# First products row by row: fc1's weights loaded in chunks over all partitions, the first two chunks multiplied for row 0 and then for row 1

## The chip, the cores and the metric

The kernel runs on one NeuronCore of one Trainium2 chip. The metric is the device time of one execution in microseconds (us); less is better. Beside it stands the span of the profile, from the first to the last instruction of the core.

## What is computed

`x` is 32 rows of 256 tokens with 256 features. Each row has an expert number. All arrays are float32.

```
h        = gelu(einsum('bnd,hd->bnh', x, fc1_w) + fc1_b)         # fc1_w: 1024 x 256
shared   = einsum('bnh,sh->bns', h, fc2_w) + fc2_b               # 192 outputs
expert_x = einsum('bnh,bph->bnp', h, experts_w[indices]) + be    # 64 outputs
return x + concatenate([shared, expert_x], axis=-1)
```

## The kernel before

**Blocks.** A block is two rows (R = 2), that is 512 tokens, and there are 16 blocks. Each fp32 operand is split into a high part (HI, written by ScalarE as fp32r) and a low part (LO, the difference, mostly written by VectorE, for the hidden values by GpSimd), and a product is three matmuls: HI x HI, HI x LO and LO x HI. fc1 of blocks 0 and 1 is computed plainly, in eight chunks of 128 hidden features (`conv_chunk`, L961, six matmuls of 512 columns each: two halves `d` of the features times three terms). From block 2 on a scheme with sums of blocks is used (L985). fc2 (`fc2_units`, L1017, L1019, L1021) takes two chunks of hidden values, a pair, at a time.

**Order.** Nothing is scheduled by a tool: each engine has its own instruction stream, written by hand, and waits on semaphores. The streams of TensorE (PE), ScalarE (ACT), VectorE (DVE), GpSimd (POOL) and SyncE (SP) are what stands in the functions below.

**The opening.** TensorE first runs `warm` (L930), products of the identity that feed nothing. It transposes block 0 of `x` (`x0_banks`, into `tr_ps`), then the first half of fc1's weights (`w1_bank(0, d)`, four chunks, into `acc_ps`), then the bias, then runs chunk 0 (`first_chunk`, L968), transposes the second half of the weights (`w1_bank(1, d)`, into `tr_ps`), and runs chunks 1 to 7 without a break. Behind them stands `fc2_units(0, 0, 0, 8)`, whose first matmul waits for the first pair of hidden values. Between TensorE's steps ScalarE splits off the high parts (`x0_high` L417, `w1_high` L430) and VectorE the low ones (`x0_low` L646, `w1_low` L659).

**The first pair of hidden values.** ScalarE applies the gelu to chunks 0 and 1 (`conv_chunk` L522; chunk 0 waits for `b1_ready`, which VectorE's copy of the transposed bias sets, L826), and later rounds the pair to its high part (`conv_high(0)`, L510). GpSimd makes the low part (`pair_lo`, L353, semaphore `h_lo`). Ahead of `conv_high(0)` ScalarE and VectorE have to get fc2's weights ready in turns: VectorE transposes a quarter (`w2_square`, L682), ScalarE writes its high part (`w2_high`, L440), VectorE its low part (`w2_low`, L690). `w2_square(0)` stands behind `w1_low(1, 1)` in VectorE's stream. After fc2's weights come the experts' weights (L701, L709) and block 1 of `x` (L720, and its low part L737, `x1_lo`), for which TensorE's `conv_chunk(K)` waits behind `fc2_units(0, 0, 0, 8)`.

**Loads.** The queue of SP issues the two rows of block 0, waits for row 0 (`x0_loaded[0]`), and issues the second half of fc1's weights, four DMAs of 32 partitions each, and then fc2's. ACT's queue issues the expert numbers, the first half of fc1's weights in the same form, and fc1's bias.

The opening of TensorE's stream in the source:

```
for d in range(D):
    w1_bank(0, d)
pe.wait_ge(b1_loaded, 16)
nc.tensor.transpose(fc1_ps[:, 3, 0:K], b1_in[:, :], ident[0:K, 0:K]).then_inc(b1_tr, 1)
first_chunk()
pe.wait_ge(w1_loaded[1], 16 * Q)
```

## Time and profile before

| | |
|---|---|
| median of 3 runs | 363.62 us (363.24 to 364.08) |
| the profiled execution's own time | 363.34 us |
| its span | 361.5 us |
| TensorE (PE) matmuls busy | 356.4 us (99%) |
| PE weight loads (PEld) busy | 350.3 us (97%) |
| ScalarE (ACT) busy | 243.6 us (67%) |
| VectorE (DVE) busy | 224.0 us (62%) |
| GpSimd (POOL) busy | 222.2 us (61%) |
| mean granted TensorE clock | 0.998 |

The profile shows one execution. Its span is 1.84 us shorter than its own time, and that time is 0.28 us under the median. Busy times of different engines overlap. A row of a timeline gives the start from the beginning of the span, the length, the engine, the line of the kernel, and what is written from what; a row with "x6" stands for six instructions in succession, and its length runs from the first start to the last end. The engine is idle ahead of an instruction where square brackets say so, and behind the arrow stands what ended the idle time.

### The profile page before, as it was taken

The page shows a single profiled execution, that of the slowest core. Times are in us where ns is not written, and L with a number is a line of the kernel's source. Part 1 is how long each engine was busy: PE and PEld are TensorE (multiplying, and loading weights), DVE is VectorE, ACT ScalarE, POOL GpSimd, SP SyncE. Part 2 cuts the span into 40 slices and gives each one's busy share as a digit, 9 for nine tenths or more (in the row PEclk, how much of TensorE's full clock was granted, in tenths as well). Part 3 has the DMA queues.
Part 4 walks back from the last instruction along what each step waited for, and adds up shares of the span by engine and source line. Part 5 has one row for each costly group of instructions (what it writes and reads, how often), then busy time and mean ns, then how long its engine had stood idle before and what let it go on. Part 6 is the DMA issues. An engine that isn't in the chain of part 4 may idle for free.

```text
span 361.5 us, 7842 instructions
## 1 busy us (share of the span) xinstructions
PE 356.4 (99%) x2863; PEld 350.3 (97%) x2863; DVE 224.0 (62%) x367; ACT 243.6 (67%) x410; POOL 222.2 (61%) x100
## 2 busy tenths in 40 slices
PE   8999999999999999999999999999999999999996
PEld 6898999999999999999999999999999999999996
DVE  1797993937758285683937658395673938653241
ACT  3794865757849576694857759576794857757560
POOL 0079824676655677565676655677565577655381
PEclk9999999999999999999999999999999999999999
DMA  8869856361703426044261603526052321403011
GB/s 202 183 160 117 156 143 150 126 160 45 175 22 116 127 69 173 31 124 89 82 160 52 168 25 109 132 82 162 29 140 74 94 91 58 126 18 100 2 58 58
DMA packets 70447, 37.86 MB, mean 105 GB/s; under 512 B 43530, under 2 KB 70410, under 8 KB 70410
## 3 DMA queue, kind: packets, MB, share of 16 engines
q1 hardware_dynamic: 69792, 36.85, 40.8%
q10 hardware_dynamic: 618, 0.53, 0.6%
q8 instruction: 22, 0.36, 0.4%
q14 instruction: 15, 0.12, 0.1%
HBM read 28.97 MB, written 8.39 MB: 103 GB/s over the span
## 4 chain that ended last, share of the span: by engine, by line
PE 95%; issue 2%; POOL 1%; ACT 1%; DVE 0%; POOLq 0%
PE fc_ps L985 37%; PE acc_ps L1017 16%; PE acc_ps L1021 16%; PE acc_ps L1019 16%; PE fc_ps L961 6%; PE fc_ps L930 1%; POOL ht L353 1%; PE tr_ps L924 1%; PE fc_ps L968 1%; ACT ht L510 0%; ACT gelu L536 0%; DVE work L794 0%; DVE resid L819 0%; ACT w1t L430 0%; PE acc_ps L924 0%
## 5 line engine op out<-in xcount | busy, mean ns | idle before, releaser
L353 POOL TENSOR_TENSOR ht<-gelu,ht 128x1024 fp32r<-128x1024 f32 x60 | 144.5, 2408 | 121.3 <-ACT ht L510 121.3
L985 PE MATMUL fc_ps<-xt,w1t 128*128 128x256 f32 x1176 | 173.2, 283 | 0.0
L985 PEld LDWEIGHTS fc_ps<-xt,w1t 128*128 128x128 f32 x1176 | 155.3, 192 | 0.1
L1017 PE MATMUL acc_ps<-w2t,ht 128*128 128x256 f32 x512 | 144.9, 283 | 0.2 <-POOL ht L353 0.2
L1019 PE MATMUL acc_ps<-w2t,ht 128*128 128x256 f32 x512 | 144.9, 283 | 0.0
L1021 PE MATMUL acc_ps<-w2t,ht 128*128 128x256 f32 x512 | 144.9, 283 | 0.0
L1017 PEld LDWEIGHTS acc_ps<-w2t,ht 128*128 128x128 f32 x512 | 98.3, 192 | 0.6 <-POOL ht L353 0.3
L1019 PEld LDWEIGHTS acc_ps<-w2t,ht 128*128 128x128 f32 x512 | 98.3, 192 | 0.3
L1021 PEld LDWEIGHTS acc_ps<-w2t,ht 128*128 128x128 f32 x512 | 98.3, 192 | 0.0
L510 ACT ACTIVATE ht<-gelu 128x1024 fp32r<-128x1024 f32 x64 | 68.0, 1062 | 3.3
L496 ACT ACTIVATE work<-fc_ps 128x512 f32<-128x512 f32 x28 | 16.8, 600 | 57.4 <-PE fc_ps L985 57.4
L778 DVE TENSOR_TENSOR work<-fc_ps,work 128x512 f32<-128x512 f32 x28 | 19.4, 691 | 54.6 <-PE fc_ps L985 45.8
L346 POOL TENSOR_TENSOR resid<-resid,bias 128x1024 f32<-128x1024 f32 x16 | 38.9, 2432 | 1.5 <-DMA resid<-in_x 0.8
L787 DVE TENSOR_TENSOR work<-fc_ps,work 128x512 f32<-128x512 f32 x28 | 19.2, 687 | 32.0 <-PE fc_ps L985 32.0
L361 POOL TENSOR_TENSOR xt<-work,xt 128x1024 fp32r<-128x1024 f32 x14 | 33.6, 2402 | 7.7 <-ACT xt L500 7.7
L450 ACT ACTIVATE w2t<-tr_ps 128x512 fp32r<-128x512 f32 x32 | 18.8, 590 | 29.0 <-PE acc_ps L1021 29.0
L536 ACT ACTIVATE gelu<-work,b 128x512 f32<-128x512 f32 x56 | 37.1, 712 | 0.7 <-DVE work L794 0.7
L794 DVE TENSOR_TENSOR work<-fc_ps,work 128x512 f32<-128x512 f32 x28 | 19.3, 691 | 12.8 <-PE fc_ps L985 11.2
L548 ACT ACTIVATE gelu<-work,b 128x256 f32<-128x256 f32 x56 | 25.2, 501 | 0.0
L709 DVE TENSOR_TENSOR w2t<-tr_ps,w2t 128x512 fp32r<-128x512 f32 x32 | 22.0, 690 | 4.7 <-ACT w2t L450 3.2
L802 DVE TENSOR_TENSOR work<-fc_ps,work 128x512 f32<-128x512 f32 x28 | 19.1, 683 | 7.2 <-PE fc_ps L985 7.2
L553 ACT ACTIVATE gelu<-fc_ps,b 128x256 f32<-128x256 f32 x56 | 23.3, 469 | 0.0
(57 smaller groups left out, 279.5 us busy)
## 6 DMA issues: line engine op xcount, KB each, us to landing
pieces<-in_L_cond_experts_w SPq DMA_DIRECT2D x128, 64.0 KB, 2.0
out<-resid SPq DMA_DIRECT2D x32, 256.0 KB, 3.0
pieces<-in_x SPq DMA_DIRECT2D x60, 128.0 KB, 3.6
resid<-in_x SPq DMA_DIRECT2D x15, 512.0 KB, 4.1
bias<-in_L_cond_experts_b SPq DMA_DIRECT2D x32, 32.0 KB, 2.9
w_piece<-in_L_cond_fc_w SPq DMA_DIRECT2D x4, 256.0 KB, 4.5
w_piece<-in_L_cond_fc_w SPq DMA_DIRECT2D x4, 192.0 KB, 5.0
resid<-in_x SPq DMA_DIRECT2D x2, 256.0 KB, 3.4
```

The costliest lines, as they stand in the source:

```text
L346: nc.gpsimd.tensor_tensor(rows, rows, bias[:, par, :, :].unsqueeze(2).to_broadcast([P, R, T, OUT]), ALU.add).then_inc(resid_ready, 1)
L353: nc.gpsimd.tensor_tensor(ht[:, slot, LO, :, :].rearrange("p k t -> p (k t)"), gelu[:, q % GELUS, :, :].rearrange("p k t -> p (k t)"), ht[ ...
L361: nc.gpsimd.tensor_tensor(xt[:, n % 2, X_T1:X_T4 + 1, LO, :], t_sum, xt[:, n % 2, X_T1:X_T4 + 1, HI, :].bitcast(FP32), ALU.subtract).then_ ...
L510: nc.scalar.activation(ht[:, q % PAIRS, HI, :, :].rearrange("p k t -> p (k t)"), gelu[:, q % GELUS, :, :].rearrange("p k t -> p (k t)"), A ...
L536: nc.scalar.activation(gelu[:, q % GELUS, j, :], upper[:, j, :], ACT.Gelu, bias=b1[:, k:k + 1]).then_inc(up_gelu, 1)
L548: nc.scalar.activation(gelu[:, q % GELUS, j, SEQ:2 * SEQ], c22[:, j, :], ACT.Gelu, bias=b1[:, k:k + 1]).then_inc(c22_gelu, 1)
L553: nc.scalar.activation(gelu[:, q % GELUS, j, 0:SEQ], fc1_ps[:, BANK_A[t % 2], j * SEQ:(j + 1) * SEQ], ACT.Gelu, bias=b1[:, k:k + 1]).then_ ...
L709: nc.vector.tensor_tensor(expert_columns(LO, ks), tr_ps[:, half, :].rearrange("p (k b c) -> p b k c", k=HALF, b=R), expert_columns(HI, ks) ...
L985: last = nc.tensor.matmul(fc1_ps[:, dst, j * SEQ:(j + 1) * SEQ], w1t[:, w, wv, ms], xt[:, n % 2, o, xv, :], start=(fresh and j == 0 and at ...
L1017: nc.tensor.matmul(dst, h_hi_t, w_hi, start=(r == 0 and u % (2 * T) == 0), stop=True, skip_group_check=True)
L1019: nc.tensor.matmul(dst, h_hi_t, w_lo, start=False, stop=True, skip_group_check=True)
L1021: last = nc.tensor.matmul(dst, h_lo_t, w_hi, start=False, stop=True, skip_group_check=True)
```

## The change

The loads of fc1's first half become four DMAs, one for each chunk, each over all 128 partitions (`load_w1_chunk`): chunks 0 and 1 from ACT's queue, chunks 2 and 3 from SP's queue, right behind block 0. The bias and the expert numbers move to SP's queue. The second half of the weights keeps its four DMAs.

A bank of transposed weights now holds two chunks with both halves of the features (`w1_bank(half, l)`), where it held four chunks with one half. A bank of transposed `x` holds one row (`x0_banks(b)`), where it held one half of the features of both. `x0_high`, `x0_low`, `w1_high` and `w1_low` follow: there are as many of them and they are as large as before, in another order. `first_chunk(c, b)` computes chunk c for row b, six matmuls of 256 columns, and runs for chunks 0 and 1, first for row 0, then for row 1. Ten of the 30 warming products are gone. On ScalarE the second of the two `w1_high` of the second half moves behind the gelu of chunk 1.

```diff
+    w1_chunks = fc1_w.rearrange("(q k c) d -> k q c d", q=Q, c=S)
...
+        def x0_row(v, b):
+            return xt0[:, :, v, b * SEQ:(b + 1) * SEQ]
+        def x0_bank(b):
+            return tr_ps[:, b, :].rearrange("p (d t) -> p d t", d=D)
+        W1_ORDER = ((0, 1), (1, 0))
+        def w1_slots(half, l, v):
+            cols = slice(2 * half * P, (2 * half + 2) * P)
+            if l == 0:
+                return w1t[:, W_A11:W_A12 + 1, v, cols]
+            return w1t[:, W_A22:W_A21 + 1:W_A21 - W_A22, v, cols]
+        def w1_rows(half, l):
+            return (acc_ps, tr_ps)[half][:, l, :].rearrange("p (d c) -> p d c", d=D)
...
+        w1_loaded = [sem(f"w1_loaded{n}") for n in range(3)]
         w1p_loaded = sem("w1p_loaded")
...
-        def load_w1(queue, half):
-            ks = slice(half * HALF, (half + 1) * HALF)
-            for q in range(Q):
-                queue.dma_start(w1_in[S * q:S * (q + 1), ks, :], w1_v[q][:, ks, :])\
-                    .then_inc(w1_loaded[half], 16)
+        def load_w1_chunk(queue, k):
+            queue.dma_start(w1_in[:, k, :], w1_chunks[k]).then_inc(w1_loaded[k // 2], 16)
...
                 sp.dma_start(resid[:, 0, ts, :], x_blocks[0][:, ts, :]).then_inc(x0_loaded[b], 16)
+            load_w1_chunk(sp, 2)
+            load_w1_chunk(sp, 3)
+            sp.dma_start(b1_in[:, :].rearrange("k (q c) -> k q c", q=Q),
+                         fc1_b.rearrange("(q k c) -> k q c", q=Q, c=S))\
+                .then_inc(b1_loaded, 16)
+            sp.dma_start(index_sb[:, :], index.rearrange("(o n) -> o n", o=1))\
+                .then_inc(index_loaded, 16)
             sp.wait_ge(x0_loaded[0], 16)
-            load_w1(sp, 1)
+            for q in range(Q):
+                sp.dma_start(w1_in[S * q:S * (q + 1), HALF:K, :], w1_v[q][:, HALF:K, :])\
+                    .then_inc(w1_loaded[2], 16)
...
-            def x0_high(d):
-                act.wait_ge(x0_tr, d + 1)
-                nc.scalar.activation(xt0[:, d, HI, :], tr_ps[:, d, :], ACT.Copy)\
-                    .then_inc(x0_hi, 1)
-            def w1_slots(half, d, v):
-                cols = slice(2 * half * P, (2 * half + 2) * P)
-                if d == 0:
-                    return w1t[:, W_A11:W_A21 + 1:W_A21 - W_A11, v, cols]
-                return w1t[:, W_A12:W_A22 + 1, v, cols]
-            def w1_high(half, d):
-                act.wait_ge(w1_tr, D * half + d + 1)
-                src = (acc_ps, tr_ps)[half][:, d, :].rearrange("p (l c) -> p l c", l=2)
-                nc.scalar.activation(w1_slots(half, d, HI), src, ACT.Copy).then_inc(w1_hi, 1)
+            def x0_high(b):
+                act.wait_ge(x0_tr, b + 1)
+                nc.scalar.activation(x0_row(HI, b), x0_bank(b), ACT.Copy).then_inc(x0_hi, 1)
+            def w1_high(half, l):
+                act.wait_ge(w1_tr, 2 * half + l + 1)
+                nc.scalar.activation(w1_slots(half, l, HI), w1_rows(half, l), ACT.Copy)\
+                    .then_inc(w1_hi, 1)
...
-            act.dma_start(index_sb[:, :], index.rearrange("(o n) -> o n", o=1))\
-                .then_inc(index_loaded, 16)
-            load_w1(act, 0)
-            act.dma_start(b1_in[:, :].rearrange("k (q c) -> k q c", q=Q),
-                          fc1_b.rearrange("(q k c) -> k q c", q=Q, c=S))\
-                .then_inc(b1_loaded, 16)
+            load_w1_chunk(act, 0)
+            load_w1_chunk(act, 1)
             act.wait_ge(ident_ready, 1)
             nc.scalar.activation(gelu[:, 0, 0, 0:1], ident[:, 0:1], ACT.Gelu)\
                 .then_inc(gelu_loaded, 1)
             act.wait_ge(gelu_loaded, 1)
-            for d in range(D):
-                x0_high(d)
-            for d in range(D):
-                w1_high(0, d)
+            x0_high(0)
+            w1_high(0, 0)
+            x0_high(1)
+            w1_high(0, 1)
             act.wait_ge(b1_ready, 1)
             conv_chunk(0)
             w1_high(1, 0)
+            conv_chunk(1)
             w1_high(1, 1)
-            conv_chunk(1)
...
-            def x0_low(d):
-                dve.wait_ge(x0_hi, d + 1)
-                nc.vector.tensor_tensor(xt0[:, d, LO, :], tr_ps[:, d, :],
-                                        xt0[:, d, HI, :].bitcast(FP32), ALU.subtract)\
-                    .then_inc(x0_lo, 1)
...
-            def w1_low(half, d):
-                dve.wait_ge(w1_hi, D * half + d + 1)
-                src = (acc_ps, tr_ps)[half][:, d, :].rearrange("p (l c) -> p l c", l=2)
-                nc.vector.tensor_tensor(w1_slots(half, d, LO), src,
-                                        w1_slots(half, d, HI).bitcast(FP32), ALU.subtract)\
+            def x0_low(b):
+                dve.wait_ge(x0_hi, b + 1)
+                nc.vector.tensor_tensor(x0_row(LO, b), x0_bank(b), x0_row(HI, b).bitcast(FP32),
+                                        ALU.subtract).then_inc(x0_lo, 1)
+            def w1_low(half, l):
+                dve.wait_ge(w1_hi, 2 * half + l + 1)
+                nc.vector.tensor_tensor(w1_slots(half, l, LO), w1_rows(half, l),
+                                        w1_slots(half, l, HI).bitcast(FP32), ALU.subtract)\
                     .then_inc(w1_lo, 1)
...
-            for d in range(D):
-                x0_low(d)
-            for d in range(D):
-                w1_low(0, d)
+            x0_low(0)
+            w1_low(0, 0)
+            x0_low(1)
+            w1_low(0, 1)
             dve.wait_ge(b1_tr, 1)
             nc.vector.tensor_copy(b1[:, :], fc1_ps[:, 3, 0:K]).then_inc(b1_ready, 1)
-            for d in range(D):
-                w1_low(1, d)
+            w1_low(1, 0)
+            w1_low(1, 1)
             w2_square(0)
...
                 pe.wait_ge(x0_loaded[b], 16)
-                for d in range(D):
-                    last = transposes(tr_ps[:, d, b * SEQ:(b + 1) * SEQ],
-                                      [feature_chunk(resid[:, 0, b * T + t, :], d)
-                                       for t in range(T)])
-                    if b == R - 1:
-                        last.then_inc(x0_tr, 1)
-            def w1_bank(half, d):
-                transposes((acc_ps, tr_ps)[half][:, d, :], [
-                    feature_chunk(w1_in[:, k, :], d)
-                    for k in range(half * HALF, (half + 1) * HALF)]).then_inc(w1_tr, 1)
+                transposes(tr_ps[:, b, :], [
+                    feature_chunk(resid[:, 0, b * T + t, :], d)
+                    for d in range(D) for t in range(T)]).then_inc(x0_tr, 1)
+            def w1_bank(half, l):
+                k = half * HALF + 2 * l
+                transposes((acc_ps, tr_ps)[half][:, l, :], [
+                    feature_chunk(w1_in[:, k + j, :], d)
+                    for d in W1_ORDER[l] for j in range(2)]).then_inc(w1_tr, 1)
...
-            def first_chunk():
-                def product(d, w, v):
-                    return nc.tensor.matmul(fc1_ps[:, 0, :], conv_operand(0, d, w), xt0[:, d, v, :],
-                                            start=(d == 0 and w == v), stop=(d == D - 1 and w == LO))
-                for d in range(D):
-                    pe.wait_ge(w1_hi, d + 1)
-                    product(d, HI, HI)
-                    pe.wait_ge(x0_lo, d + 1)
-                    product(d, HI, LO)
-                for d in range(D):
-                    pe.wait_ge(w1_lo, d + 1)
-                    last = product(d, LO, HI)
-                last.then_inc(conv_filled, 1)
+            def first_chunk(c, b):
+                for at, (w, v, d) in enumerate([(w, v, d) for w, v in ((HI, HI), (HI, LO), (LO, HI))
+                                                for d in range(D)]):
+                    if c == 0 and at == 0:
+                        pe.wait_ge(w1_hi, 1)
+                        pe.wait_ge(x0_hi, b + 1)
+                    if c == 0 and (w, v, d) == (HI, LO, 0):
+                        pe.wait_ge(x0_lo, b + 1)
+                    if c == 0 and (w, v, d) == (LO, HI, 0):
+                        pe.wait_ge(w1_lo, 1)
+                    last = nc.tensor.matmul(fc1_ps[:, c, b * SEQ:(b + 1) * SEQ],
+                                            conv_operand(c, d, w),
+                                            xt0[:, d, v, b * SEQ:(b + 1) * SEQ],
+                                            start=(b == 0 and at == 0), stop=True,
+                                            skip_group_check=True)
+                if b == R - 1:
...
             warm(WARM)
-            for b in range(R):
-                x0_banks(b)
-            warm(WARM // 2)
-            pe.wait_ge(w1_loaded[0], 16 * Q)
-            for d in range(D):
-                w1_bank(0, d)
+            x0_banks(0)
+            pe.wait_ge(w1_loaded[0], 32)
+            w1_bank(0, 0)
+            x0_banks(1)
+            first_chunk(0, 0)
             pe.wait_ge(b1_loaded, 16)
             nc.tensor.transpose(fc1_ps[:, 3, 0:K], b1_in[:, :], ident[0:K, 0:K]).then_inc(b1_tr, 1)
-            first_chunk()
-            pe.wait_ge(w1_loaded[1], 16 * Q)
-            for d in range(D):
-                pe.wait_ge(x0_lo, d + 1)
-                w1_bank(1, d)
-            conv_chunk(1)
+            first_chunk(1, 0)
+            pe.wait_ge(w1_loaded[1], 32)
+            w1_bank(0, 1)
+            first_chunk(0, 1)
+            first_chunk(1, 1)
+            pe.wait_ge(w1_loaded[2], 16 * Q)
+            pe.wait_ge(x0_lo, 1)
+            w1_bank(1, 0)
+            pe.wait_ge(x0_lo, 2)
+            w1_bank(1, 1)
+            pe.wait_ge(w1_lo, 2)
             conv_chunk(2)
             conv_chunk(3)
-            pe.wait_ge(w1_lo, 4)
+            pe.wait_ge(w1_lo, 3)
             conv_chunk(4)
             conv_chunk(5)
+            pe.wait_ge(w1_lo, 4)
             conv_chunk(6)
             conv_chunk(7)
```

TensorE's stream from its start to the first fc2 matmul, before (`w_in` is fc1's weights as loaded, `w1t` the split weights, `resid` block 0 of `x`; in these rows `tr_ps`, `acc_ps` and `fc_ps` are PSUM banks):

```order
L930 MATMUL fc_ps<-ident 128x256 x20
L924 MATMUL tr_ps<-ident,resid 128x128 x8
L930 MATMUL fc_ps<-ident 128x256 x10
L924 MATMUL acc_ps<-ident,w_in 128x128 x8
L1037 MATMUL fc_ps<-ident,b_in 128x8
L968 MATMUL fc_ps<-xt,w1t 128x512 x6
L924 MATMUL tr_ps<-ident,w_in 128x128 x8
L961 MATMUL fc_ps<-xt,w1t 128x512 x42
```

The same place in the changed kernel:

```order
L937 MATMUL fc_ps<-ident 128x256 x20
L931 MATMUL tr_ps<-ident,resid 128x128 x4
L931 MATMUL acc_ps<-ident,w_in 128x128 x4
L931 MATMUL tr_ps<-ident,resid 128x128 x4
L982 MATMUL fc_ps<-xt,w1t 128x256 x6
L1046 MATMUL fc_ps<-ident,b_in 128x8
L982 MATMUL fc_ps<-xt,w1t 128x256 x6
L931 MATMUL acc_ps<-ident,w_in 128x128 x4
L982 MATMUL fc_ps<-xt,w1t 128x256 x12
L931 MATMUL tr_ps<-ident,w_in 128x128 x8
L966 MATMUL fc_ps<-xt,w1t 128x512 x36
```

The first half of the weights is now transposed in two parts: one ahead of row 1 of `x`, the other behind the products of chunks 0 and 1 for row 0. 24 products of 256 columns take the place of 12 of 512, and 36 products of 512 stand ahead of fc2 where 42 stood.

ScalarE's stream from its first instruction on block 0 to its first on fc2's weights (L440, in the changed kernel L459), before:

```order
L417 ACTIVATE xt<-tr_ps 128x512 [waits x0_tr,gelu_loaded]
L417 ACTIVATE xt<-tr_ps 128x512 [waits x0_tr]
L430 ACTIVATE w1t<-acc_ps 128x2x256 [waits w1_tr] x2
L522 ACTIVATE gelu<-fc_ps,b 128x512 [waits conv_filled,b1_ready]
L430 ACTIVATE w1t<-tr_ps 128x2x256 [waits w1_tr] x2
L522 ACTIVATE gelu<-fc_ps,b 128x512 [waits conv_filled]
L440 ACTIVATE w2t<-acc_ps 128x2x192 [waits w2_sq] x2
```

The same place in the changed kernel:

```order
L444 ACTIVATE xt<-tr_ps 128x2x256 [waits x0_tr,gelu_loaded]
L448 ACTIVATE w1t<-acc_ps 128x2x256 [waits w1_tr]
L444 ACTIVATE xt<-tr_ps 128x2x256 [waits x0_tr]
L448 ACTIVATE w1t<-acc_ps 128x2x256 [waits w1_tr]
L541 ACTIVATE gelu<-fc_ps,b 128x512 [waits conv_filled,b1_ready]
L448 ACTIVATE w1t<-tr_ps 128x2x256 [waits w1_tr]
L541 ACTIVATE gelu<-fc_ps,b 128x512 [waits conv_filled]
L448 ACTIVATE w1t<-tr_ps 128x2x256 [waits w1_tr]
L459 ACTIVATE w2t<-acc_ps 128x2x192 [waits w2_sq] x2
```

Ahead of the first gelu stand the same four instructions in another order; the gelu of chunk 1 now stands between the two `w1_high` of the second half. VectorE's stream changes only in the order of its first four instructions; the copy of the bias (L826) still stands behind them, and `w1_low` of the second half behind the copy.

## Rows read from the trace of the kernel before

**Rows 1.** The page: the span, and busy time of each engine

```profile
span 361.5 us, 7842 instructions
PE 356.4 (99%) x2863; PEld 350.3 (97%) x2863; DVE 224.0 (62%) x367; ACT 243.6 (67%) x410; POOL 222.2 (61%) x100
```

**Rows 2.** PE busy (x), clock, DMA share, GB/s from 44 to 345 us

```profile
44.00:345.00 301.00, 301.00 (x2509) 1.00 0.36 98
```

**Rows 3.** Timeline of PE, the opening

```profile
1.53 4.12 PE L930 MATMUL fc_ps<-ident 128*128 128x256 bf16 x20 [1.53 <-POOL ident L379]
5.49 1.12 PE L924 MATMUL tr_ps<-ident,resid 128*128 128x128 f32 x8
6.45 1.25 PE L930 MATMUL fc_ps<-ident 128*128 128x256 bf16 x10
...
8.59 0.22 PE L1037 MATMUL fc_ps<-ident,b_in 8*128 8x8 f32 x1
8.86 1.83 PE L968 MATMUL fc_ps<-xt,w1t 128*128 128x512 f32 x6
```

**Rows 4.** Timeline of PEld: first half's end, fc2's first load, chunk 8's first

```profile
11.36 9.42 PEld L961 LDWEIGHTS fc_ps<-xt,w1t 128*128 128x128 f32 x42
20.82 0.19 PEld L1017 LDWEIGHTS acc_ps<-w2t,ht 128*128 128x128 f32 x1
...
23.80 0.19 PEld L961 LDWEIGHTS fc_ps<-xt,w1t 128*128 128x128 f32 x1
```

**Rows 5.** Timeline of POOL: the low part of the first pair

```profile
18.16 2.41 POOL L353 TENSOR_TENSOR ht<-gelu,ht 128x1024 fp32r<-128x1024 f32 x1 [16.68 <-ACT ht L510]
```

**Rows 6.** Timeline of DVE, the opening

```profile
7.10 0.69 DVE L646 TENSOR_TENSOR xt<-tr_ps,xt 128x512 fp32r<-128x512 f32 x1 [7.10 <-ACT xt L417]
...
10.05 0.16 DVE L826 COPY b<-fc_ps 128x8 f32<-128x8 f32 x1
12.00 1.29 DVE L659 TENSOR_TENSOR w1t<-tr_ps,w1t 128x512 fp32r<-128x512 f32 x2 [1.80 <-ACT w1t L430]
13.21 1.04 DVE L682 STREAM_TRANSPOSE acc_ps<-w_piece 128x384 f32<-128x384 f32 x2
...
22.86 0.68 DVE L737 TENSOR_TENSOR xt<-tr_ps,xt 128x512 fp32r<-128x512 f32 x1
```

**Rows 7.** Timeline of ACT, the opening

```profile
6.47 0.60 ACT L417 ACTIVATE xt<-tr_ps 128x512 fp32r<-128x512 f32 x1 [1.44 <-PE tr_ps L924]
...
10.79 0.69 ACT L522 ACTIVATE gelu<-fc_ps,b 128x512 f32<-128x512 f32 x1 [1.49 <-PE fc_ps L968]
11.38 1.08 ACT L430 ACTIVATE w1t<-tr_ps 128x512 fp32r<-128x512 f32 x2
...
13.82 0.95 ACT L440 ACTIVATE w2t<-acc_ps 128x384 fp32r<-128x384 f32 x2
...
17.02 1.06 ACT L510 ACTIVATE ht<-gelu 128x1024 fp32r<-128x1024 f32 x1
```

**Rows 8.** Timeline of SP's queue, DMAs issued

```profile
0.75 0.95 SPq L286 DMA_DIRECT2D resid<-in_x  x2
3.76 1.76 SPq L236 DMA_DIRECT2D w_in<-in_L_cond_fc_w  x4
5.57 1.93 SPq L291 DMA_DIRECT2D w_piece<-in_L_cond_fc_w  x4
```

**Rows 9.** DMA issues to 40 us (median us to landing); GB/s of each us

```profile
GB/s 0 18 239 321 296 238 237 237 234 214 236 212 246 149 217 235 105 44 115 215 188 155 125 86 128 162 243 239 188 200 152 57 56 53 55 78 148 156 214 167
...
w_piece<-in_L_cond_fc_w SPq DMA_DIRECT2D x4, 192.0 KB, 5.0
resid<-in_x SPq DMA_DIRECT2D x2, 256.0 KB, 3.4
w_in<-in_L_cond_fc_w ACTq DMA_DIRECT2D x4, 128.0 KB, 4.1
```

**Rows 10.** The chain that ended last: six products of 256 columns

```profile
45.90 0.72 PE fc_ps L985 x6
```

More of the change, by code:

```diff
@@ L120, in cond_mlp_residual @@
         stored = [sem(f"stored{n}") for n in range(2)]
-        w1_loaded = [sem(f"w1_loaded{n}") for n in range(2)]
+        w1_loaded = [sem(f"w1_loaded{n}") for n in range(3)]
         w1p_loaded = sem("w1p_loaded")
@@ L964, in conv_chunk @@
                 last.then_inc(conv_filled, 1)
-            def first_chunk():
-                def product(d, w, v):
-                    return nc.tensor.matmul(fc1_ps[:, 0, :], conv_operand(0, d, w), xt0[:, d, v, :],
-                                            start=(d == 0 and w == v), stop=(d == D - 1 and w == LO))
-                for d in range(D):
-                    pe.wait_ge(w1_hi, d + 1)
-                    product(d, HI, HI)
-                    pe.wait_ge(x0_lo, d + 1)
-                    product(d, HI, LO)
-                for d in range(D):
-                    pe.wait_ge(w1_lo, d + 1)
-                    last = product(d, LO, HI)
-                last.then_inc(conv_filled, 1)
+            def first_chunk(c, b):
[14 more added lines that the diff above has]
+                if b == R - 1:
+                    last.then_inc(conv_filled, 1)
             def product(n, g, dst, w, o, fresh):
```

5 lines of the change are left out of this document (removed).

## The prediction

> **What bounds the kernel now.** I read the page first. TensorE is busy 99% of a span of 361.5 us, and no other engine more than 67% [rows 1]. The windows say where the missing 1% is not: from 44 to 345 us TensorE is busy for all 301 us at the full clock [rows 2]. The change touches only the first 12 us or so. So whatever it does must move the moment at which TensorE comes into that full stretch, and the time of the kernel moves by as much. TensorE's timeline of the opening comes next [rows 3]: it cannot start before 1.53 us, it warms itself for 4.12 us, transposes from 5.49, fills 1.25 us with ten more warming products, and the first product that counts begins at 8.86. That is the hole that the change works on.
>
> The question then is who is late next. TensorE's weight loads show chunks 1 to 7 from 11.36 for 9.42 us, so to 20.78, and the first load of fc2 at 20.82, with no wait shown [rows 4]. But what that fc2 matmul waits for, `h_lo`, comes from GpSimd's instruction at 18.16 of 2.41 us, which ends at 20.57 [rows 5]. The margin is 0.25 us. The next wait, chunk 8 on `x1_lo`, is as tight: the load stands at 23.80 [rows 4], VectorE's last low part ends at 22.86 + 0.68 = 23.54 [rows 6]. Two chains run side by side here, TensorE's own and that of ScalarE, VectorE and GpSimd, and they meet within 0.25 us.
>
> What sets the second chain is read on VectorE and ScalarE. From 13.21 VectorE and ScalarE work by turns on fc2's weights: ScalarE's first copy of them is at 13.82, after the first of VectorE's two transposes from 13.21 [rows 6, 7]. At 17.02, 3.81 us after 13.21, ScalarE rounds the first pair, in 1.06 us, and at 18.16 GpSimd begins [rows 5, 7]. The products that these steps need are long finished: chunks 1 to 3 take 18 of the 42 loads from 11.36. So I call T the start of `w2_square(0)`, 13.21 us; `h_lo` follows at T + 7.36 and `x1_lo` at T + 10.33. T itself follows from the gelu of chunk 0 at 10.79: 0.59 later ScalarE's first high part (11.38), 0.62 later VectorE's first low part (12.00), and two of those at a pitch of 0.60 give 13.21 [rows 6, 7].
>
> **The change, the loads.** SP issued one DMA of a row in about 0.47 us and had issued its first of fc1's second half at 3.76, when row 0 had landed; fc2's weights follow at 5.57 to 7.50 [rows 8]. Four more DMAs of about 0.45 fit between 1.70 and 3.5, so SP's queue is hardly later, and ACT's has four fewer. fc2's weights take 5.0 us to land [rows 9], so they are there by about 12.5, or 13 if all slips by half a microsecond, and T' below is later than that. Chunks 0 and 1 are issued by about 1.65; such a DMA took 4.1 us with four of them in the queue [rows 9], so both land by about 5.3 where 5.97 is wanted. The GB/s row says the same by bytes: 874 KB had moved by 5 us (18 + 239 + 321 + 296), and row 0 with the two chunks is 512 KB. I cost the loads at nothing.
>
> The Trainium skill ("DMA: Bandwidth & Descriptors", Issuing engines are not separate DMA queues) says that DMAs of all issuing engines run on the same 16 DMA engines and interleave, so that two queues save issue time only. No row here splits the two, and the sum goes by the bytes.
>
> **TensorE's new opening**, step by step. Eight transposes took 1.12 us and the next work began 0.96 after their start, so a pitch is 0.12 and one lasts 0.28; the first copy on ScalarE (6.47) came 0.10 after the sixth, the last that it needs [rows 3, 7]. A product of 256 columns costs 0.12 (six in 0.72) [rows 10], one of 512 costs 9.42 / 42 = 0.224 [rows 4]. ScalarE: 0.60 a copy, pitch 0.49; VectorE: 0.69, pitch 0.60, and 0.03 after ScalarE (6.47 + 0.60 to 7.10) [rows 6, 7].
>
> Row 0's four transposes from 5.49 end at 6.13, ScalarE's `x0_high(0)` starts at 6.23. The four of chunks 0 and 1 end at 6.61, `w1_high(0, 0)` runs from 6.72 to 7.31. TensorE has transposed row 1 by 7.1 and starts its first product at about 7.35, 1.5 us before the old one. VectorE: `x0_low(0)` at 6.86, `w1_low(0, 0)` from 7.46 to 8.15. TensorE waits for that ahead of its fifth product, does two until 8.43, the bias (between 0.12 and 0.22 by its length [rows 3]; I take 0.14), and the six of chunk 1 until 9.29. Only now come the transposes of chunks 2 and 3, which before were done in one go with the others: the last ends at 9.29 + 0.36 + 0.28 = 9.93.
>
> **TensorE's side.** From 9.29: four transposes (0.48), 12 products (1.44), eight transposes (0.96) give 12.17 for the start of chunk 2. Before, it was 11.36 + 6 x 0.224 = 12.70. TensorE gains 0.55 us and would be at fc2 at 20.27. In it the split of 12 products of 512 columns into 24 of 256 costs 24 x 0.12 - 12 x 0.224 = 0.2.
>
> **The other side.** ScalarE's `w1_high(0, 1)` starts at 10.03, ends 10.63; VectorE's `w1_low(0, 1)` 10.66; the copy of the bias stands behind it, 0.60 later as before, at 11.26, and takes 0.16 [rows 6]. Only then may ScalarE start the gelu of chunk 0: 11.45, where it was 10.79. 0.59 later the first high part of the second half, 12.04; 0.49 later the gelu of chunk 1, which now stands between the two, 12.53; 0.59 later the second high part, 13.12 to 13.72; VectorE's last `w1_low` 13.75, and T' = 14.35. That is 1.14 after T: 0.66 from the bias standing behind a late bank, 0.48 from the gelu in between.
>
> **Sum.** `h_lo` at 20.57 + 1.14 = 21.71, so fc2 starts at about 21.75 instead of 20.82: +0.93. TensorE will have waited some 1.5 us for it. `x1_lo` at 23.54 + 1.14 = 24.68 against 23.80 + 0.93 = 24.73 adds nothing. The hand-overs may be a few hundredths shorter, as PE to ScalarE; I take +0.9. On the profiled execution: 363.34 + 0.9 = 364.24. That execution was 0.28 below the median of the three, 363.62, and against the median the number is **364.5 us**. The bounds of the parts (bias, hand-overs, an unseen wait for the high parts in the queue of ScalarE) make 364.1 to 364.9 for this case. A measurement of this kernel tells some 0.2% (0.73 us) from no change, so the forecast lies only a little above that bound.
>
> **The rivals.**
> - *The turns have slack (0.20).* ScalarE's and VectorE's steps behind T may absorb some of the 1.14, or the bias comes earlier than I have it. For it: the interval of 3.81 us is more than any one engine's work in it. Against: the copy at 13.82 follows its transpose within hundredths. With half of the delay gone, 0.57 - 0.25 = +0.3: 363.9 us, and no change to be measured.
> - *TensorE's gain is kept (0.07): faster.* If `h_lo` came by 20.23, fc2 would start at 20.27 and the kernel would take 363.62 - 0.55 = 363.1. This decides only if T' is 12.87 or earlier, 1.5 us before what I work out. For it: the first product starts 1.5 us earlier. Against: the gelu of chunk 0 is the gate, and that waits for the bias copy.
> - *Late chunks (0.07).* Chunks 0 and 1 now compete with row 0 from the start. If they land at 6.7 instead of before 5.97, all steps shift by 0.7: 365.2. For it: row 0 itself took 3.4 us [rows 9]. Against: the bytes above. In this case the change does not do what it says, since no product starts much before 8.1.
> - *The clock (0.06).* Twenty warming products took 4.12 us, ten later ones 1.25 [rows 3]: a pitch of 0.2 against 0.11, so 1.2 GHz first and 2.4 GHz later, after TensorE had been working. Ten warming products are gone and a wait of 1.5 us is new. If the clock fell in that wait and the next twenty products of 256 columns ran at the lower level, as twenty did at the start, each would cost 0.09 more: +1.8, in all 366.3. Against: waits of some tenths in the old opening left no slow product behind, but none was as long. The Trainium skill ("TensorE: Matmul & The Clock Gate", Part 1: The HAM clock gate) says that an idle TensorE goes back to 1.2 GHz and activity releases it; the trace agrees on the release at the start, and shows no fall.
>
> **The numbers.** Forecast 0.60, slack 0.20, gain kept 0.07, late chunks 0.07, clock 0.06. The range from 363.3 to 365.5 leaves out the kept gain, the clock and a part of the late chunks. Of the forecast's 0.60 about 0.42 lies above +0.73 us, with the late chunks and the clock slower has 0.56; faster has 0.08; the rest, 0.36, is the same.
>
> **What would show it.** In the changed profile: the first product near 7.35, chunk 2 near 12.2, the gelu of chunk 0 near 11.45, the transpose of fc2's weights near 14.35, an idle time of about 1.5 us on TensorE ahead of fc2's first load with GpSimd's low part as its releaser, and the full stretch from there on as before. I would be wrong if that idle time is missing, if the gelu of chunk 0 starts before 11 us, or if the wait for `w1_loaded` stands in the opening.

## The result, and the profile after

The changed kernel takes 372.68 us (median of 4 runs, 372.25 to 372.75), the kernel before in the same session 363.82 (363.24 to 364.08). The ratio is 1.0243, with a 95% interval from 1.0226 to 1.0261: 8.9 us slower. I had forecast slower, by 0.9 us. The direction holds, and the size is wrong by a factor of ten.

The page of the changed kernel, to be read against [rows 1]:

```profile
span 370.5 us, 7849 instructions
PE 357.9 (97%) x2865; PEld 351.7 (95%) x2865; DVE 224.0 (60%) x367; ACT 243.5 (66%) x410; POOL 223.2 (60%) x100
PEclk9699999999999999999999999999999999999999
```

TensorE's busy time grew by 1.5 us, the span by 9.0. So TensorE waits, and the clock line says where: in the second slice, which ends at 18.5 us. The waits of TensorE in the changed kernel, the two lists of PEld and PE (engine, what it waited for, total, times, longest):

```profile
PEld acc_ps L931 <- DMA w_in<-in_L_cond_fc_w: 6.6, 1, 6.6
PEld acc_ps L1027 <- POOL ht L380: 1.9, 2, 1.6
...
PE acc_ps L931 <- DMA w_in<-in_L_cond_fc_w: 6.3, 1, 6.3
```

The first line is new. TensorE waits 6.6 us for chunks 0 and 1 to land. The second is the wait that I had forecast at 1.5 us; its longest is 1.6. The timeline of the changed kernel, against [rows 3 to 7]:

```profile
0.74 1.72 ACTq L255 DMA_DIRECT2D w_in<-in_L_cond_fc_w  x2
...
1.75 1.32 SPq L255 DMA_DIRECT2D w_in<-in_L_cond_fc_w  x2
...
5.78 0.91 PE L931 MATMUL tr_ps<-ident,resid 128*128 128x128 f32 x4
...
13.02 0.73 PEld L931 LDWEIGHTS acc_ps<-ident,w_in 128*128 128x128 f32 x4 [6.58 <-DMA w_in<-in_L_cond_fc_w]
...
19.55 0.69 ACT L541 ACTIVATE gelu<-fc_ps,b 128x512 f32<-128x512 f32 x1 [0.83 <-PE fc_ps L982]
...
20.19 2.85 PEld L966 LDWEIGHTS fc_ps<-xt,w1t 128*128 128x128 f32 x13
...
22.43 1.04 DVE L689 STREAM_TRANSPOSE acc_ps<-w_piece 128x384 f32<-128x384 f32 x2
...
27.39 2.39 POOL L380 TENSOR_TENSOR ht<-gelu,ht 128x1024 fp32r<-128x1024 f32 x1 [25.90 <-ACT ht L529]
...
29.82 0.19 PEld L1027 LDWEIGHTS acc_ps<-w2t,ht 128*128 128x128 f32 x1 [1.57 <-POOL ht L380]
```

Both loads on ACT's queue were issued by 2.46 us, and TensorE could start on them at 13.0. The four transposes of row 0 are done by 6.7, and between the two TensorE does nothing. The windows of PE in the changed kernel (busy (x), granted clock, DMA share, GB/s) show the two other things that matter, what the DMA engines did and what the clock did:

```profile
3.00:4.00 1.00, 1.00 (x6) 1.00 0.89 293
4.00:5.00 1.00, 1.00 (x7) 1.00 0.28 98
5.00:6.00 1.00, 1.00 (x7) 1.00 0.53 140
...
8.00:10.00 2.00, 0.00 (x0) 0.96 1.08 203
10.00:12.00 2.00, 0.00 (x0) 0.50 1.09 182
12.00:14.00 2.00, 0.98 (x5) 0.50 0.34 72
14.00:16.00 2.00, 2.00 (x10) 0.50 0.28 76
16.00:18.00 2.00, 2.00 (x15) 0.84 0.54 153
```

Between 4 and 5 us all four chunk loads are under way, and yet the sixteen DMA engines are busy only 28% of the time and move 98 GB/s; the kernel before moved 296 [rows 9], at a share of 1.13:

```profile
4.00:5.00 1.00, 1.00 (x7) 1.00 1.13 296
```

Queues that have work and engines that idle: the work is on few of them. And after some microseconds without a matmul the granted clock falls to 0.50, which is 1.2 GHz; it is back in the window from 16 to 18 (0.84 on average, so at about 16.6), that is, it stays low for the first 3.6 us of real work.

### The profile page after: what moved, and what is told of

It reads as the page before. It is cut to its first block, busy times and chain, and to the rows that moved or that the text cites. A ratio compares the mean times of both kernels' runs of the same rounds, so it can differ in the third digit from the quotient of the medians.

```text
span 370.5 us, 7849 instructions
## 1 busy us (share of the span) xinstructions
PE 357.9 (97%) x2865; PEld 351.7 (95%) x2865; DVE 224.0 (60%) x367; ACT 243.5 (66%) x410; POOL 223.2 (60%) x100
## 4 chain that ended last, share of the span: by engine, by line
PE 89%; DMA 3%; issue 2%; POOL 2%; ACT 2%; DVE 1%; ACTq 0%; DVEq 0%; POOLq 0%
PE fc_ps L995 37%; PE acc_ps L1027 16%; PE acc_ps L1031 16%; PE acc_ps L1029 16%; PE fc_ps L966 3%; DMA w_in<-in_L_cond_fc_w 3%; POOL ht L380 2%; PE fc_ps L982 1%; ACT ht L529 1%; ACT gelu L541 0%; PE acc_ps L931 0%; ACT w2t L459 0%; DVE acc_ps L689 0%; ACTq L255 0%; ACT w1t L448 0%
## 5 line engine op out<-in xcount | busy, mean ns | idle before, releaser
L373 POOL TENSOR_TENSOR resid<-resid,bias 128x1024 f32<-128x1024 f32 x16 | 39.7, 2481 | 0.0
```

The lines of the kernel that those rows point to most:

```text
L373: nc.gpsimd.tensor_tensor(rows, rows, bias[:, par, :, :].unsqueeze(2).to_broadcast([P, R, T, OUT]), ALU.add).then_inc(resid_ready, 1)
```

## The experiments

**Theories.** A: the source of a chunk load has four steps in its outermost dimension (`k q c d`, q = 4), and such a DMA runs on four of the sixteen engines only. All four chunks pile up there, and whatever else passes these engines waits with them. B: ACT's queue is starved while SP's queue has a backlog (SP no longer pauses behind the two rows). C: a DMA over 128 partitions of this kind is slow in itself.

**e1_quarters: the loads in the old form.** The computation stays as changed.

```diff
-        def load_w1_chunk(queue, k):
...
-            queue.dma_start(w1_in[:, k, :], w1_chunks[k]).then_inc(w1_loaded[k // 2], 16)
+        def load_w1_pair(queue, l):
+            ks = slice(2 * l, 2 * l + 2)
+            for q in range(Q):
+                queue.dma_start(w1_in[S * q:S * (q + 1), ks, :], w1_v[q][:, ks, :])\
+                    .then_inc(w1_loaded[l], 16)
...
```

Pair 0 comes from ACT's queue and pair 1 from SP's, and TensorE waits for 64 where it waited for 32; the same holds for every kernel below that loads in this form.

> The changed kernel, but chunks 0 and 1 come from ACT's queue and chunks 2 and 3 from SP's as four DMAs of 32 partitions x 2 chunks each, the form that the kernel before uses, in place of one DMA of 128 partitions per chunk. Theory A (the new form of the chunk loads has four steps in its outermost source dimension and so runs on four of the sixteen DMA engines): the loads land by about 5.5 us, the wait of 6.3 us is gone, and what is left is the predicted lateness of the chain of ScalarE, VectorE and GpSimd: 364.5 us (364.1 to 364.9), with the gelu of chunk 0 near 11.5 and fc2's first load near 21.7. Theory B (ACT's queue is starved while SP's queue has a backlog, whatever the form): chunks 0 and 1 still land near 12 to 13 us, 371 to 373 us.

Measured: 365.0 us (364.73 to 365.36, 10 runs), ratio 1.0032 (1.0021 to 1.0044), against a before of 363.88. 7.7 of the 8.9 us are gone by the form of four loads alone. B as it stands is out, since the queues and the bytes in them are the same. What is left is 0.32% or 1.2 us; it is mostly my chain, which e6_sixteen below shows with the loads on time, but TensorE still waits 0.87 us for the chunks here and starts on them at 6.34, where I had 5.97. The timeline of e1_quarters:

```profile
6.34 0.56 PEld L931 LDWEIGHTS acc_ps<-ident,w_in 128*128 128x128 f32 x4 [0.87 <-DMA w_in<-in_L_cond_fc_w]
...
12.02 0.69 ACT L542 ACTIVATE gelu<-fc_ps,b 128x512 f32<-128x512 f32 x1 [0.83 <-PE fc_ps L982]
12.60 0.59 ACT L449 ACTIVATE w1t<-tr_ps 128x512 fp32r<-128x512 f32 x1
12.66 8.06 PEld L966 LDWEIGHTS fc_ps<-xt,w1t 128*128 128x128 f32 x36
...
14.90 1.04 DVE L689 STREAM_TRANSPOSE acc_ps<-w_piece 128x384 f32<-128x384 f32 x2
...
22.29 0.19 PEld L1027 LDWEIGHTS acc_ps<-w2t,ht 128*128 128x128 f32 x1 [1.56 <-POOL ht L381]
```

Against the changed kernel the first transposes of chunks come 13.02 - 6.34 = 6.68 us earlier. From there to chunk 2 it takes 12.66 - 6.34 = 6.32 us, where the changed kernel took 20.19 - 13.02 = 7.17: another 0.85, which is the slow clock (e8_warm50 tests this). Together that is 7.5, and the spans differ by 7.6.

**e2_before_chunk_form: the new form in the old kernel.** Nothing else changes.

```diff
-            load_w1(act, 0)
+            for k in range(HALF):
+                act.dma_start(w1_in[:, k, :], w1_chunks[k]).then_inc(w1_loaded[0], 16)
```

> The kernel before, with nothing changed but the form of the loads of fc1's first half: four DMAs from ACT's queue, one for each chunk over 128 partitions, in place of four of 32 partitions x 4 chunks. 
Measured: 374.25 us (4 runs), ratio 1.0286 (1.0266 to 1.0305). The form costs the old kernel 10.4 us by itself, though SP's queue paused as ever, and B allowed 1 us: as the whole cause it is out a second time. The size was above my 367.5 to 369. The wait list of e2_before_chunk_form, a window, the clock line of its page and two rows of its timeline:

```profile
PEld acc_ps L926 <- DMA w_in<-in_L_cond_fc_w: 8.3, 1, 8.3
```

```profile
4.00:5.00 1.00, 1.00 (x7) 1.00 0.14 48
```

```profile
PEclk9789999999999999999999999999999999999999
```

```profile
16.58 1.59 PEld L926 LDWEIGHTS acc_ps<-ident,w_in 128*128 128x128 f32 x8 [8.31 <-DMA w_in<-in_L_cond_fc_w]
...
21.94 4.21 PEld L963 LDWEIGHTS fc_ps<-xt,w1t 128*128 128x128 f32 x19
```

I had left two things out. The first is the clock. In the kernel before the transposes of the first half start at 7.43 us and chunk 1 at 11.36 [rows 4], 3.93 later; here it is 21.94 - 16.58 = 5.36, and the clock line is below 9 in the second and third slice (9.3 to 27.9 us). The start is 9.15 later and the stretch 1.43 longer, together the 10.6 by which the spans differ. The second is that I had counted only the chunks and block 0 on the four engines. But if SP's later loads, fc1's second half and fc2's weights, use all sixteen, they pass through these four as well, and ACT's loads share with them. The changed kernel shows the sharing in the packets of ACT's queue (q10; number, MB, share of the engines), from 4 to 5, 5 to 6 and 8 to 9 us. SP issued the second half from 4.27 on:

```profile
q10 hardware_dynamic: 63, 0.06, 18.1%
...
q10 hardware_dynamic: 18, 0.01, 4.4%
...
q10 hardware_dynamic: 28, 0.03, 15.0%
```

So a part of B is true: SP's backlog does slow ACT's loads, but in e1_quarters, where they are not on few engines, it did not make them late by more than 0.4 us. How much of the delay the sharing makes was not tried by itself.

**e3_only_act_quarters: only chunks 0 and 1 in the old form.** Chunks 2 and 3 on SP's queue stay as changed.

```diff
-            load_w1_chunk(act, 0)
-            load_w1_chunk(act, 1)
+            for q in range(Q):
+                act.dma_start(w1_in[S * q:S * (q + 1), 0:2, :], w1_v[q][:, 0:2, :])\
+                    .then_inc(w1_loaded[0], 16)
```

> The changed kernel with chunks 0 and 1 on ACT's queue in four DMAs of 32 partitions, and chunks 2 and 3 on SP's queue left as one DMA of 128 partitions each. Theory A (four engines): chunks 0 and 1 land by about 5.5 to 6 us; chunks 2 and 3 share engines with the rows and land at about 9 us, where they are wanted at 9.3; the second half stands behind them on the same engines and may be 0 to 1.5 us late: 364.5 to 366. Theory B (starved behind SP's backlog): SP's queue is as in the changed kernel, so chunks 0 and 1 still land near 12 to 13 us: 371 to 373.

Measured: 368.13 us (366.32 to 369.19, 4 runs), ratio 1.0124 (1.0102 to 1.0145). B's 371 to 373 is missed, and so are A's 364.5 to 366. In the profiled execution, the fastest of the four at 366.32, TensorE waited 0.6 us for chunks 0 and 1, and for the bias, 4 KB behind the two chunk loads in SP's queue, 1.0 us:

```profile
PEld fc_ps L1047 <- DMA b_in<-in_L_cond_fc_b: 1.0, 1, 1.0
PEld acc_ps L932 <- DMA w_in<-in_L_cond_fc_w: 0.6, 1, 0.6
```

Two of the four chunk loads are enough to be felt, and by the small loads behind them too. The other three executions took 367.8 to 369.2 us with a mean granted clock of 0.995, where the profiled one has 1.000, so a stretch at the low clock is a part of their time. What they waited for was not profiled.

**e6_sixteen and e7_eight: the number of steps.** Destination, bytes, rows of 1 KB, queue and order are those of the changed kernel. Only the source is cut otherwise: 128 steps in the outermost dimension, or eight. fc1's rows then come in another order than the bias and fc2's weights want, so these two leave the function of the reference and serve for the time alone.

```diff
-    w1_chunks = fc1_w.rearrange("(q k c) d -> k q c d", q=Q, c=S)
+    w1_chunks = fc1_w.rearrange("(k p) d -> k p d", p=P)               # e6_sixteen
+    w1_chunks = fc1_w.rearrange("(e k c) d -> k e c d", e=8, c=16)     # e7_eight
```

> The changed kernel with only the source of the four chunk loads altered: each chunk takes 128 rows of fc1_w that lie together, so that the source has 128 steps in its outermost dimension and not four. Destination, bytes, rows of 1 KB, queue and order stay. The hidden features come in another order than the bias and fc2's weights want, so the output is not the reference's. Theory A (the outermost source dimension of four confines such a DMA to four engines): as e1_quarters, 364.7 to 365.4 us, no wait for the chunks beyond about 1 us. Theory C (a DMA of 128 partitions issued this way is slow in itself, or ACT's queue gets too small a share): as the changed kernel, 372 to 373 us.

> As e6_sixteen, but the source of each chunk has eight steps in its outermost dimension, of 16 rows each (again another order of the hidden features, so the output is not the reference's). Theory A: eight engines carry the chunk loads, half as many packets on each as with four: the chunks land between those of e6_sixteen (about 6 us) and those of the changed kernel (13 us), at 7 to 9.5 us; TensorE waits 0.5 to 2.5 us, the clock hardly falls; 365.5 to 368.5 us. Theory C: 372 to 373 us.

A chunk of the changed kernel is made of four groups of 32 rows of fc1's weights, one of e7_eight of eight groups of 16, spread as widely, and in e6_sixteen the 128 rows lie together. If it mattered how the rows are scattered in memory, and not how many steps there are, e7_eight should be no faster than the changed kernel.

Measured: e6_sixteen 364.8 us, ratio 1.0029 (1.0019 to 1.0039, 9 runs); e7_eight 366.89 us, ratio 1.0099 (1.0076 to 1.0121, 4 runs). C is out, since the shape of the destination stayed. The windows of e7_eight and then of e6_sixteen, in the microsecond in which the changed kernel had a DMA share of 0.28:

```profile
4.00:5.00 1.00, 1.00 (x7) 1.00 0.57 184
```

```profile
4.00:5.00 1.00, 1.00 (x7) 1.00 1.06 361
```

Four steps give a share of 0.28, eight 0.57, 128 steps 1.06: about 4, 8 and 16 parts of sixteen. The GB/s follow, 98, 184 and 361, and so does the time. In the changed kernel all four chunk loads were under way in that microsecond, so they are on the same few engines; spread over different ones they would show a share near 1.

The pages show the same without a window. In these kernels ACT's queue carries nothing but chunks 0 and 1, 256 rows of 1 KB, as two loads, and in e1_quarters as four. Its line in the pages of the changed kernel, e7_eight, e6_sixteen and e1_quarters, in this order:

```profile
q10 hardware_dynamic: 264, 0.26, 0.3%
...
q10 hardware_dynamic: 272, 0.26, 0.3%
...
q10 hardware_dynamic: 288, 0.26, 0.2%
...
q10 hardware_dynamic: 320, 0.26, 0.3%
```

Beyond the 256 packets of rows stand 8, 16, 32 and 64 more: 4, 8 and 16 for each load, and 16 for each load of the old form. Read as one closing packet from each engine that takes part, these are the engines of each load. The Trainium skill ("DMA: Bandwidth & Descriptors", Why a DMA increments its semaphore by 16 and not by 1) has the rule: a DMA uses as many engines as the largest number up to 16 that divides the sizes of the slowest dimension (other than one) of both its sides. For 128 partitions and a source of 4 x 32 x 256 that is four. By that rule, the trace agrees in all three forms.

**e8_warm50: what the slow clock cost.** The changed kernel with its slow loads, and TensorE kept at work while it waits.

```diff
             x0_banks(0)
+            warm(50)
             pe.wait_ge(w1_loaded[0], 32)
```

> The changed kernel with 50 more warming products behind the transposes of row 0, which keep TensorE busy for about 5.5 us of the wait for chunks 0 and 1. The loads are untouched, so the chunks land at 13 us as before; if the clock then stays at 2.4 GHz, the stretch from the first transposed chunk to chunk 2 takes 6.3 us as in e1_quarters and not 7.2: 0.9 us less than the changed kernel, 371.8 us. If the slower clock cost nothing there, 372.7 us.

Measured: 371.52 us (4 runs), ratio 1.0225 (1.0205 to 1.0244), against 1.0243. The timeline of e8_warm50:

```profile
12.88 0.56 PEld L931 LDWEIGHTS acc_ps<-ident,w_in 128*128 128x128 f32 x4 [0.71 <-DMA w_in<-in_L_cond_fc_w]
...
19.20 3.30 PEld L966 LDWEIGHTS fc_ps<-xt,w1t 128*128 128x128 f32 x15
```

The clock line of its page, where the changed kernel had a 6 in the second slice:

```profile
PEclk9999999999999999999999999999999999999999
```

The clock stayed up (0.999 on average over the span), and the stretch takes 6.32 us again, as in e1_quarters, and not 7.17. The two intervals overlap, so the time alone would not settle it; the timeline does. The spans, 369.5 against 370.5, differ by these 0.85 and the 0.14 by which the chunks came earlier.

**e4_gelu_behind and e5_order_restored: the two halves of my 1.14 us.** Both start from e1_quarters. e4 puts ScalarE's order back, e5 also moves the bias.

```diff
             w1_high(1, 0)
+            w1_high(1, 1)
             conv_chunk(1)
-            w1_high(1, 1)
...
-            w1_low(0, 1)
             dve.wait_ge(b1_tr, 1)
             nc.vector.tensor_copy(b1[:, :], fc1_ps[:, 3, 0:K]).then_inc(b1_ready, 1)
+            w1_low(0, 1)
```

The lines behind the "..." are e5's alone.

> e1_quarters with two places of the order changed: ScalarE's second high part of the second half again ahead of the gelu of chunk 1, and VectorE's copy of the bias ahead of the low part of chunks 2 and 3 instead of behind it. My chain (h_lo waits for the start of w2_square, that for the gelu of chunk 0 and the two high parts): the gelu of chunk 0 then waits for the end of chunk 0 for both rows, near 10.6 us, which is 0.8 to 0.9 earlier, and the gelu of chunk 1 no longer stands between, 0.5 less: w2_square(0) at 13.1 instead of 14.35, fc2's first load at 20.5 instead of 21.7: 1.2 us less than e1_quarters, 363.3 us, a little under the kernel before. Rival (the turns on fc2's weights have slack, so that the chain is not what TensorE waits for): no difference from e1_quarters beyond 0.2 us.

> e1_quarters with ScalarE's second high part of the second half put back ahead of the gelu of chunk 1; the copy of the bias stays where the change has it. In e1_quarters the first of these high parts starts at 12.60 us, 0.14 after TensorE has its bank ready, so the bias has almost nothing to give there, and the gelu in between costs 0.5. If so this kernel takes 0.4 to 0.6 us less than e1_quarters and is equal to e5_order_restored within 0.2 us: 364.4 to 364.6. If both places counted as in my prediction (0.66 for the bias, 0.48 for the gelu) it would stand halfway, and e5_order_restored would be lower than it by 0.6.

Measured: e5_order_restored 364.53 us, ratio 1.0016 (1.0006 to 1.0026, 12 runs), and then e4_gelu_behind, ratio 1.0014 (1.0005 to 1.0023, 11 runs; its median of 364.74 stands against a before of 364.12). Against e1_quarters the order on ScalarE gives 0.5 us by the medians and 0.18%, some 0.6 us, by the ratios, whose intervals just touch. The timeline of e4_gelu_behind settles it:

```profile
12.14 0.69 ACT L542 ACTIVATE gelu<-fc_ps,b 128x512 f32<-128x512 f32 x1 [0.83 <-PE fc_ps L982]
...
21.95 0.19 PEld L1027 LDWEIGHTS acc_ps<-w2t,ht 128*128 128x128 f32 x1 [1.10 <-POOL ht L381]
```

From the gelu of chunk 0 to fc2's first load it takes 21.95 - 12.14 = 9.81 us, where e1_quarters took 22.29 - 12.02 = 10.27: 0.46 less. The bias copy gives nothing on top. My 1.2 us for both together was wrong: e5's timeline shows what I had missed.

```profile
12.12 1.03 PEld L931 LDWEIGHTS tr_ps<-ident,w_in 128*128 128x128 f32 x8
...
12.91 1.08 ACT L449 ACTIVATE w1t<-tr_ps 128x512 fp32r<-128x512 f32 x2 [0.45 <-PE tr_ps L931]
```

ScalarE waits 0.45 us for TensorE's transposes of the second half, which now stand behind the products of row 1. With the bias out of the way TensorE's own order is the next gate. In e1_quarters these transposes had been ready only 0.14 us before ScalarE took them (the first bank at 11.82 + 3 x 0.12 + 0.28 = 12.46, ScalarE at 12.60), so moving the bias could give no more than that.

**e9_banks_first: that gate opened.** e5_order_restored, with the transposes ahead of row 1's products and ScalarE's two high parts ahead of the gelu of chunk 0.

```diff
             w1_bank(0, 1)
-            first_chunk(0, 1)
-            first_chunk(1, 1)
             pe.wait_ge(w1_loaded[2], 16 * Q)
             pe.wait_ge(x0_lo, 1)
             w1_bank(1, 0)
             pe.wait_ge(x0_lo, 2)
             w1_bank(1, 1)
+            first_chunk(0, 1)
+            first_chunk(1, 1)
...
+            w1_high(1, 0)
+            w1_high(1, 1)
             act.wait_ge(b1_ready, 1)
             conv_chunk(0)
-            w1_high(1, 0)
-            w1_high(1, 1)
             conv_chunk(1)
```

> e5_order_restored with the transposes of the second half of the weights moved ahead of the 12 products of row 1, and ScalarE's two high parts of the second half ahead of the gelu of chunk 0. In e5_order_restored ScalarE waited 0.45 us for these transposes, so that TensorE's order and not ScalarE's set the start of w2_square. The products take 1.44 us: w2_square(0) at about 13.4 instead of 14.74, after which TensorE's own work (fc2's first load would come at 21.1 instead of 22.1) is the later of the two: 1.0 us less than e5_order_restored, 363.5 us, 0.3 to 0.4 under the kernel before. Rival (the loads of the second half, or row 1's bank, are late for the earlier transposes): no gain, 364.5 us.

Measured: 363.83 us (12 runs), ratio 1.0003 (0.9993 to 1.0013). fc2's first load stands at 20.73 us and no longer waits, and the kernel is equal to the one before, not better. Against e5_order_restored that is 0.5 us by the ratios and 0.7 by the medians, so half to two thirds of the 1.0 us that I expected.

**e10_split_loads and e11_warm16: further.** e10 shares the quarters of both pairs between the queues; e11 is e10 with fewer warming products.

```diff
-            load_w1_pair(act, 0)
+            load_w1_pair(act, 0, (0, 1))
+            load_w1_pair(act, 1, (0, 1))
...
                 sp.dma_start(resid[:, 0, ts, :], x_blocks[0][:, ts, :]).then_inc(x0_loaded[b], 16)
-            load_w1_pair(sp, 1)
+                load_w1_pair(sp, b, (2, 3))
...
-            warm(WARM)
+            warm(16)
```

> e9_banks_first with the quarters of the first half's loads shared out: two quarters of chunks 0 and 1 from ACT's queue and two from SP's behind row 0, then the same for chunks 2 and 3 with row 1. In e9_banks_first TensorE waited 0.8 us for chunks 0 and 1, whose fourth DMA was issued at 2.3 to 2.7 us; now the last is issued at about 2.1. 0.3 to 0.5 us less than e9_banks_first where the clock rises early, nothing where it rises late: 363.3 to 363.7 us. If row 1, now issued later, or the low part of the first pair (it had 0.3 us of margin) takes over: 363.8, no gain.

> e10_split_loads with 16 warming products in place of 20. Profiles so far show the 20 ending between 5.0 us (clock up at 4.2) and 6.0 us (clock up at 6.8); where it rises late four fewer save up to 0.8 us of time that row 0 has been there; where it rises early the chunks are not there yet and nothing is saved. 0 to 0.4 us less than e10_split_loads: 363.0 to 363.5.

Measured: e10_split_loads 364.93 us, ratio 1.0020 (1.0008 to 1.0033, 10 runs); e11_warm16 364.75 us, ratio 1.0008 (0.9996 to 1.0021, 11 runs; its median stands 0.63 us above the before of 364.12, so the ratio on record is lower than that of the medians, 1.0017). Neither gains on e9_banks_first, and e10_split_loads is slower than it. In e10's profile TensorE waits 0.9 us for row 1 instead of for the chunks, as feared, and a wait appears far behind the opening. First the timeline of GpSimd in e9_banks_first, then that in e10_split_loads:

```profile
39.03 2.68 POOL L374 TENSOR_TENSOR resid<-resid,bias 128x1024 f32<-128x1024 f32 x1 [0.67 <-DMA bias<-in_L_cond_fc_b]
```

```profile
40.41 4.87 POOL L374 TENSOR_TENSOR resid<-resid,bias 128x1024 f32<-128x1024 f32 x2 [1.99 <-DMA bias<-in_L_cond_fc_b]
```

The load of fc2's bias lands later here, and at 50 to 53 us TensorE waits twice, 1.0 us in all, for VectorE's sums. That the one leads to the other by way of GpSimd and VectorE is read from the order of events and was not tried by itself. Nor is it shown that sharing out the loads is what makes the bias late. The profile of e4_gelu_behind, whose loads are not shared out, has a late bias and a wait of the same kind, in GpSimd's timeline and in the wait list of PEld:

```profile
41.08 2.42 POOL L374 TENSOR_TENSOR resid<-resid,bias 128x1024 f32<-128x1024 f32 x1 [1.16 <-DMA bias<-in_L_cond_fc_b]
```

```profile
PEld fc_ps L995 <- DVE work L794: 0.6, 1, 0.6
```

Why e10_split_loads and e11_warm16 gain nothing stays open.

## Why the prediction was right and wrong

**The loads: wrong, and this is the step that failed.** "I cost the loads at nothing", because "such a DMA took 4.1 us with four of them in the queue" and because 874 KB had moved by 5 us. The first number belongs to DMAs of 32 partitions with a source of 32 steps, the second to these and the two rows of block 0, whose source has 128 steps. I carried them to a DMA of the same bytes in another form, and the form decides on how many engines it runs: 4, 8 or 16 by the shares 0.28, 0.57 and 1.06. The loads landed at 13.0 us, 7.7 after the 5.3 that I gave them. Of the 8.9 us they make 7.7, by e1_quarters; its timeline accounts for 7.5, of which 6.7 is the later start and 0.85 the slow clock. The prediction had named the sign, a wait for `w1_loaded` in the opening, and it came.

**The rival of late chunks: the right place, a wrong size.** I gave it 0.07 and 0.7 us, by competition with row 0. With the chunks on all sixteen engines TensorE started on them 0.37 us later than I had it in e1_quarters (6.34 for 5.97) and earlier in e6_sixteen (5.70), so the competition that I meant costs less than that. On four engines it was 6.7 and more.

**The clock rival: the mechanism was real, its occasion another.** The clock did not fall in the wait of 1.6 us ahead of fc2 in any profile taken. It fell in the 6.6 us that the loads caused, and it cost 0.85 us where I had priced 1.8 by twenty slow products. That the trace before shows no fall was misread, too. It has one at the very end: the clock is 0.58 on average from 360 to 361 us, and TensorE's last product ended at 358.2.

**The chain behind it: right.** Where the loads are on time and nothing else differs, in e6_sixteen, the chain ran as worked out: the gelu of chunk 0 at 11.57 (I had 11.45), `w2_square(0)` at 14.46 (14.35), fc2's first load at 21.85 (21.75), with a wait of 1.57 for GpSimd (1.5). The time was 0.29% over the kernel before, 1.05 us for my 0.9. The turns had no slack. The timeline of e6_sixteen:

```profile
11.57 0.69 ACT L541 ACTIVATE gelu<-fc_ps,b 128x512 f32<-128x512 f32 x1 [0.83 <-PE fc_ps L982]
...
14.46 1.04 DVE L689 STREAM_TRANSPOSE acc_ps<-w_piece 128x384 f32<-128x384 f32 x2
...
21.85 0.19 PEld L1027 LDWEIGHTS acc_ps<-w2t,ht 128*128 128x128 f32 x1 [1.57 <-POOL ht L380]
```

**The two terms of 1.14 us: the sum right, its parts not independent.** 0.48 for the gelu in between was right: 0.46 in the timelines of e1_quarters and e4_gelu_behind, 0.5 to 0.6 us in the times. The 0.66 for the late bias was real as a delay, but could not be won back by moving the bias (e5 against e4: nothing), because TensorE's transposes, which the next step needs as well, had been ready only 0.14 us earlier.

**TensorE's own gain: right in the profile, worth nothing.** With the loads on time chunk 2 started at 12.22 in e6_sixteen (12.17), and TensorE waited the gain away at fc2.

## What to carry to other kernels

- Before a DMA's price is carried from one form to another, look at the outermost dimension of both its sides. A partition pattern that is made of four groups gives a source of four steps and a quarter of the engines; the DMA share in a window shows it (0.28 where it was 1.13). One window alone can mislead: e10_split_loads, all in the old form, has 0.64 from 4 to 5 us. The queue's packet count (264, 272 or 288 for the same 256 rows) has no such doubt.
- Loads that stand in a queue behind one on few engines are late too, however small: 1.0 us for 4 KB of bias in e3_only_act_quarters. TensorE's clock may fall on top.
- A gain ahead of a wait with 0.25 us of margin is worth 0.25 us at most. Work out the second chain first; and when one gate on it is moved, look at the next, which here had opened only 0.14 us before the first.

## What the runs showed of the hardware that was not expected

- The DMAs of few source steps also took longer to issue. Two of four steps took 1.72 us on ACT's queue and 1.32 on SP's; two of eight steps, in e7_eight, 1.89 and 1.44; two of 128 steps, in e6_sixteen, 0.91 and 0.93. Four of the old form took 1.80 on ACT's queue in the kernel before.
- The opening differs between executions by the moment at which TensorE's clock rises. The windows read 1.00 there throughout; the rise is read from the pace of the products: in e1_quarters 10 stand in the window from 4 to 5 us, in the changed kernel 7. The 20 warming products took 3.64 us in e1_quarters, 4.12 in the kernel before [rows 3] and 4.45 in the changed kernel. The four transposes of row 0 behind them took 0.64 to 1.06 us. Openings of two single profiles therefore compare only to within about 1 us.
